# Identity products in TensorE's waits, at five places of a two-layer decoder kernel

## The reference

```
x = x + five SSM layers and one causal attention (16 heads of 64) of layernorm(x)
x = x + cross-attention (16 heads of 16) of layernorm(x) with the context
x = x + mixture of 8 experts, the two best of each token, of layernorm(x)
x = x + single-head self-attention of layernorm(x)
x = x + single-head cross-attention with four layernorms
x = x + int8-quantised product of layernorm(x) with a 256x256 matrix
```

## Time and profile before

| | us |
|---|---|
| median of three runs | 1249.07 (1248.18 to 1254.14) |
| profiled execution | 1250.04 |
| its span, first to last instruction | 1248.2 |
| TensorE matmul busy | 1113.7 (89%), 7155 records |
| VectorE busy | 795.8 (64%) |
| ScalarE busy | 707.1 (57%) |
| GpSimd busy | 714.3 (57%) |

### The profile page before, as it was taken

The page is one execution under the profiler, slowest core; times in us unless marked ns, Lnnn a source line. Parts: engine busy times, 40 slices in busy tenths (PEclk is TensorE's granted clock), DMA queues, the critical chain, the costliest instruction groups (busy, mean ns, idle before and its releaser), DMA issues.

```text
span 1248.2 us, 21861 instructions
## 1 busy us (share of the span) xinstructions
PE 1113.7 (89%) x7155; PEld 879.0 (70%) x7155; DVE 795.8 (64%) x1827; ACT 707.1 (57%) x2030; POOL 714.3 (57%) x776
## 2 busy tenths in 40 slices
PE   3999999999969999999988599984799999977983
PEld 3888888888857888888866477763466666656762
DVE  6778887888843666666675588876332333314795
ACT  2768777777833655555554588880223443225873
POOL 3598898989760225243353677760467555642664
PEclk9999999999989999999999899995899999998995
DMA  4201010000002000000020124610622222221001
GB/s 149 124 18 31 18 12 28 8 29 18 17 1 68 1 2 1 2 1 2 2 60 10 60 88 143 254 35 17 154 43 46 47 44 43 44 44 58 1 26 43
DMA packets 40225, 55.87 MB, mean 45 GB/s; under 512 B 8416, under 2 KB 35040, under 8 KB 38592
## 3 DMA queue, kind: packets, MB, share of 16 engines
q1 hardware_dynamic: 31392, 44.38, 10.9%
q0 software_dynamic: 8736, 10.25, 5.2%
HBM read 42.88 MB, written 11.74 MB: 44 GB/s over the span
## 4 chain that ended last, share of the span: by engine, by line
PE 45%; issue 7%; ACT 7%; DVE 7%; POOL 3%; DMA 1%; POOLq 0%; ACTq 0%; DVEq 0%
PE bank L1577 11%; PE bank L1594 5%; ACT x_prob L1244 4%; PE bank L44 4%; PE bank L46 3%; PE bank L45 3%; PE bank L704 2%; PE bank L732 2%; PE bank L715 2%; PE bank L1334 1%; PE bank L1586 1%; PE bank L1347 1%; PE bank L1284 1%; PE bank L2063 1%; POOL a_prob L871 1%
## 5 line engine op out<-in xcount | busy, mean ns | idle before, releaser
L440 DVE SCALAR_TENSOR_TENSOR ssm_conv<-bank,conv_w,ssm_conv 128x508 f32<-128x508 f32 (+2 forms) x240 | 160.8, 732 | 27.5 <-ACT ssm_conv L356 27.5
L765 ACT ACTIVATE a_prob<-a_prob,a_neg_max 128x128 f32<-128x128 f32 x256 | 99.7, 391 | 117.8 <-DVE a_neg_max L811 117.8
L1577 PE MATMUL bank<-expert_raw,x_kept_next_t 128*128 x312 | 148.7, 600 | 1.2 <-ACT x_kept_next_t L1656 1.2
L871 POOL TENSOR_TENSOR a_prob<-a_prob,a_inv 128x512 f32<-128x512 f32 x64 | 66.5, 1040 | 138.9 <-DVE a_inv L816 138.9
L552 POOL TENSOR_TENSOR ssm_u_lo<-ssm_conv,ssm_u_hi 128x512 fp32r<-128x512 f32 x80 | 101.4, 1289 | 27.0 <-ACT ssm_conv L366 26.9
L1521 POOL DMA_INDIRECT x_rows<-e_y,e_index x39 | 62.9, 1612 | 75.6 <-ACT e_y L1684 71.9
L1244 ACT ACTIVATE x_prob<-bank,x_neg_max 128x128 f32<-128x128 f32 x256 | 89.7, 401 | 11.5 <-DVE x_neg_max L1221 11.5
L1800 DVE COPY e_h_t<-bank 128x512 f32<-128x512 f32 x39 | 27.0, 691 | 105.4 <-PE bank L1586 105.4
L44 PE MATMUL bank<-w_out_hi,ssm_u_hi 128*128 128x256 f32 x320 | 92.1, 288 | 1.1 <-POOL ssm_u_lo L552 1.1
L1131 POOL TENSOR_TENSOR x_prob<-x_prob,x_inv 128x512 f32<-128x512 f32 x64 | 67.0, 1052 | 42.0 <-DVE x_inv L1225 41.5
L46 PE MATMUL bank<-w_out_hi,ssm_u_lo 128*128 128x256 f32 x320 | 90.8, 284 | 0.0
(11 more groups left out here) (338 smaller groups left out, 3264.4 us busy)
## 6 DMA issues: line engine op xcount, KB each, us to landing
expert_raw<-in_experts_laid SPq DMA_DIRECT2D x8, 1536.0 KB, 8.2
attn_raw<-in_attn_w_laid SPq DMA_DIRECT2D x1, 4096.0 KB, 12.4
w_in_raw<-in_L_attn_in_proj_w SPq DMA_DIRECT2D x5, 640.0 KB, 5.9
w_out_raw<-in_L_attn_out_proj_w SPq DMA_DIRECT2D x5, 512.0 KB, 3.9
x_res<-in_x SPq DMA_DIRECT2D x4, 512.0 KB, 5.5
x_res<-in_x SPq DMA_DIRECT2D x1, 2048.0 KB, 8.7
x_context<-in_ctx_t_laid SPq DMA_DIRECT2D x8, 256.0 KB, 4.0
z_rows<-x_kept_next_z SPq DMA_DIRECT2D x8, 256.0 KB, 2.2
```

What stands on the lines that cost most here:

```text
L440: op = dve.scalar_tensor_tensor(out=acc, in0=xs, scalar=conv_w[:, c, TAPS - 1 - back:TAPS - back], in1=acc, op0=ALU.mult, op1=ALU.add)
L765: e = act.activation(prob[:, m % 4, i, :], prob[:, m % 4, i, :], ACT.Exp, bias=neg_max[:, m % 4, i:i + 1], accum_out=total[:, m % 4, i:i + 1])
L871: pool.tensor_tensor(prob[:, t % 4, :, :], prob[:, t % 4, :, :], inv[:, t % 4, :].unsqueeze(2).broadcast_to([P, 4, P]), ALU.mult).then_inc ...
L1577: mm = pe.matmul(bank[:, :], rows_t[:, t % 2, k, :], W[:, bass.ds(at + (column + k * FFN), FFN)], start=(k == 0), stop=(k == KD - 1))
```

## The change

A function multiplies the 128x128 identity by itself, so many times, into a PSUM bank that nobody reads at that point. TensorE calls it at these places: after the attention outputs of tick 64 (8 products, with a wait for all masked scores ahead) and after the output projection of unit 30 (9); after the scores of the first cross-attention sequence (20, with a wait for the attention's sums ahead); in routing after the last sequence's probability transposes of r = 2 (4), its output projection (14), the last pair's transposes (3) and logits (18), the ranks (32) and the sum (26); at the hand-over after the three prepared products (18) and at the start of the second layer's block (21); and, by a table, after eight phases of the last pairs. Nothing else is changed: no other instruction is moved or removed, and no other engine's program differs.

```
--- before.py
+++ after.py
@@ -595,6 +595,13 @@
 WIDE = HEADS * HEAD
 KW = WIDE // P
 OCT = KW // 2
+
+
+def keep_at_work(pe, mem, bank, products):
+
+    ident = mem["ident"]
+    for _ in range(products):
+        pe.matmul(mem["psum"][bank][:, 0:P], ident[:, :], ident[:, :], start=True, stop=True)
 
 
 def stage_self_attention(nc, ctx, io, mem):
@@ -733,6 +740,9 @@
                                        v[:, s, head * HEAD:(head + 1) * HEAD], prob_t[:, (t - 1 + par) % 4, i, :],
                                        start=True, stop=True, tile_position=(0, par * HEAD))
                 mm.then_inc(ot_ready, 1)
+                if m == TICKS:
+                    pe.wait_ge(masked, TICKS)
+                    keep_at_work(pe, mem, 0, 8)
             unit = behind(m, OUT)
             if unit:
                 U, G, octet, s = unit
@@ -742,6 +752,8 @@
                     mm = product(pe, Y(U), [o_t_hi[:, U % 2, c, :], o_t_lo[:, c, :]], [x[:, octet * OCT + c, :] for x in wo],
                                  c == 0, c == OCT - 1)
                 mm.then_inc(y_ready, 1)
+                if U == TICKS // 2 - 2:
+                    keep_at_work(pe, mem, 0, 9)
             for half, j in jobs_at(m):
                 job(half, j)
             following(pe, m)
@@ -1309,6 +1321,8 @@
                     for s in range(PAIR):
                         tr = pe.transpose(psum[6][:, k * PT + s * P:k * PT + (s + 1) * P], next_z[:, s, k * P:(k + 1) * P], ident[:, :])
                 tr.then_inc(next_turned, 1)
+                if n == PAIRS - 1:
+                    keep_at_work(pe, mem, 3, 3)
             elif phase == "logits":
                 if n == 0:
                     pe.wait_ge(router_loaded, 16)
@@ -1318,6 +1332,8 @@
                         mm = pe.matmul(psum[6][:, s * EXPERTS:(s + 1) * EXPERTS], next_t[:, k, s * P:(s + 1) * P],
                                        router[:, k * EXPERTS:(k + 1) * EXPERTS], start=(k == 0), stop=(k == KD - 1))
                 mm.then_inc(logits_ready, 1)
+                if n == PAIRS - 1:
+                    keep_at_work(pe, mem, 3, 18)
             elif phase == "scores":
                 G, s = divmod(n, PAIR)
                 pe.wait_ge(k_copied, G + 1)
@@ -1336,6 +1352,9 @@
                                        tile_position=(r * ROWT, 0))
                         if c == KD - 1:
                             mm.then_inc(s_ready[r], 1)
+                if n == 0:
+                    pe.wait_ge(attention["y_added"], 2 * SEQS - 1)
+                    keep_at_work(pe, mem, 6, 20)
             elif phase == "turn_probs":
                 pe.wait_ge(prob_ready[r], n + 1)
                 copied = n * PAIR + r // 2
@@ -1346,6 +1365,8 @@
                 for i in range(4):
                     tr = pe.transpose(PT_BANK[r % 2][:, i * P:(i + 1) * P], prob[:, n % 2, r, i, :], ident[:, :])
                 tr.then_inc(pt_ready[r], 1)
+                if n == SEQS - 1 and r == 2:
+                    keep_at_work(pe, mem, 3, 4)
             elif phase == "outputs":
                 G, s = divmod(n, PAIR)
                 pe.wait_ge(v_copied, G + 1)
@@ -1370,6 +1391,8 @@
                 for k in range(KD):
                     mm = pe.matmul(Y, o[:, k, :], wo[:, k, :], start=(k == 0), stop=(k == KD - 1))
                 mm.then_inc(y_ready, 1)
+                if n == SEQS - 1:
+                    keep_at_work(pe, mem, 3, 14)
 
     phases = {
         "tensor": ("project_k", "project_v", "turn_z", "project_q", "scores", "turn_probs", "outputs", "project_o", "turn_next", "logits"),
@@ -1548,6 +1571,7 @@
                            either[:, b, :].unsqueeze(1).broadcast_to([P, SEQS - b, EXPERTS]),
                            start=False, stop=(b == SEQS - 1), skip_group_check=True)
         mm.then_inc(rank_ready, 1)
+        keep_at_work(pe, mem, 3, 32)
 
         pe.wait_ge(token_seq, 1)
         pe.wait_ge(token_lane, 1)
@@ -1556,6 +1580,7 @@
             mm = pe.matmul(SUM, lane_hot[:, n, :], token[:, n, :, :].rearrange("p a t -> p (a t)"),
                            start=(n == 0), stop=(n == CHOICES * SEQS - 1))
         mm.then_inc(sum_ready, 1)
+        keep_at_work(pe, mem, 3, 26)
 
         def turn_rows(t):
             pe.wait_ge(gathered[t % 3], 16 * (t // 3) + 16)
@@ -1637,6 +1662,7 @@
         for c in range(KD):
             mm = pe.matmul(SCALES[:, c * P:(c + 1) * P], ones[:, :], diag[:, c, :], start=True, stop=True)
         mm.then_inc(scales_ready, 1)
+        keep_at_work(pe, mem, 0, 18)
 
     def scalar(act):
         act.wait_ge(route_exp, 1)
@@ -1886,6 +1912,8 @@
     (456, "invert_o"), (462, "gain_o"), (475, "add_o"), (493, "norm_f"), (499, "measure_f"), (505, "invert_f"), (531, "scale_f"),
     (532, "quantise"), (532, "turn_f"), (544, "copy_f"), (571, "multiply"), (583, "store"), (675, "add_f"))}
 APART = 60
+BETWEEN = {("cscores", PAIRS - 2): 14, ("turn_cprobs", PAIRS - 2): 4, ("cscores", PAIRS - 1): 5, ("turn_cprobs", PAIRS - 1): 7,
+           ("multiply", PAIRS - 3): 10, ("turn_f", PAIRS - 2): 3, ("multiply", PAIRS - 2): 22, ("turn_f", PAIRS - 1): 2}
 
 
 def in_turn(*phases):
@@ -2047,6 +2075,7 @@
                     mm = pe.matmul(bank[:, s * D:(s + 1) * D], probs_t[:, s, :], vs(s), start=True, stop=True)
                 mm.then_inc(ready, 1)
 
+            keep_at_work(pe, mem, 0, 21)
             for phase, G in in_turn("turn_a", "project_q", "project_v", "scores", "turn_probs", "outputs", "turn_x", "cscores",
                                     "turn_cprobs", "coutputs", "turn_f", "multiply"):
                 if phase == "turn_a":
@@ -2114,6 +2143,7 @@
                             mm = pe.matmul(F[:, s * D:(s + 1) * D], xq_t[:, k * PAIR + s, :], wfq_t[:, k, :],
                                            start=(k == 0), stop=(k == KD - 1))
                     mm.then_inc(fy_ready, 1)
+                keep_at_work(pe, mem, 1, BETWEEN.get((phase, G), 0))
 
         @block.scalar
         def _(act):
```

## The result

The changed kernel takes 1241.64 us (median of five runs, 1241.41 to 1243.51), the kernel before 1249.41 us (five runs, 1248.18 to 1254.14). The ratio is 0.9932 with a 95% interval of 0.9914 to 0.995: faster by 0.7%, some 8 us, where some 13 us were forecast. The profiled execution has a span of 1239.7 us, 8.5 us less than before, and a mean granted clock of 0.985.

A forecast was written before the change was run, and what follows sets the result against it. Dependency chains in which PE takes its turns at 1.2 GHz were taken as the bound, ceiling 22.4 us. Terms 1.7 + 0 + 4.8 + 2.8 + 3.9 = 13.2 us gave a forecast of 1236.5 us, range 1231 to 1246.

The forecast's parts named there:

- rival (a): Whole kernel: every clock fall is only delayed or shortened, about half the gain is left, 6 us: 1243; chance 0.19.
- the price of a product: All fills: one product is two records, 0.22 us at 2.4 GHz and 0.44 us at 1.2 GHz.
- rival (c): All fills: records into one bank do not overlap, 0.55 us a product, some 50 us slower: 1300; chance 0.02.
- (e): Whole kernel: the products do not count for the clock, or PE is busy anyway; no change, 1249; chance 0.06.
- Self-attention's end: 8 and 9 products before 675.6 and 691.0: the half-clock stretch 676.75 to 680.17 vanishes, 1.7 us gained.
- hand-over: Between the layers, 18 and 21 products: transposes, query projection and value projection at full clock, 2.8 us gained.
- First scores: First cross-attention scores, 20 products: the clock falls a few microseconds later, is not spared, and the gain is 0.
- Routing: Six fills from outputs to gather: 3.2 us from shortened turns, 0.4 from ranks, 1.2 behind the sum, 4.8 us.
- the doubt: Routing behind the sum: thin PE work may let the clock fall, so the 26 products overrun; 1.2 of 2.2 us taken.
- The end of the second layer: Eight fills at the last pairs: transposes, outputs and last multiply at full clock, 1.7 + 1.3 + 0.9 = 3.9 us.
- (b): Routing from 844 on: fills begin at 1.2 GHz and overrun; +10 us, 1260; chance 0.08.
- (d): Whole kernel: the clock holds everywhere, 698 and 869 included, 15.8 us gained, 1234; chance 0.20.

The follow-up runs named there:

- scores_more: Changed kernel with 29 instead of 20 products behind the first cross-attention scores and 2 more behind each of the first two probability-transpose groups; 1239.75 us, ratio 0.9918.
- light_add: Changed kernel with GpSimd's last residual addition of pairs 3 and 4 done on 8 of 256 columns; 1238.9 us, ratio 0.9893.
- sum_fill: Changed kernel with two more products behind each of the first three groups of eight summing matmuls in routing; 1243.54 us, ratio 0.9938.
- the mends: Changed kernel plus products inside the sum, more at the first scores and second layer's start, and GpSimd's last additions later; all together 1232.37 us, ratio 0.9859.
- no_end: Changed kernel without the eight fills at the end of the second layer; 1242.78 us, ratio 0.9932.
- no_26: Changed kernel without the 26 products behind the routing's sum; 1244.4 us, ratio 0.994.
- add_late: Changed kernel with GpSimd's last additions moved behind its share of the output norm, and a third buffer; 1236.67 us, ratio 0.9885.
- no_end_add_late: Changed kernel with GpSimd's last additions moved late and without the eight fills at the second layer's end; 1239.11 us, ratio 0.9901.
- all_mended_2: Changed kernel with all four mends, and two end fills enlarged (9 for 5 and 20 for 10 products); 1232.93 us, ratio 0.9859.

## Why the prediction was right, and where it was not

**The number.** By the medians 7.8 us were won, where 12.6 us were forecast (1236.5). 1241.64 us lies nearer to rival (a), 1243, than to the forecast. The range of 1231 to 1246 held it, since it was drawn to hold (a) too. What was right is the mechanism and the terms up to the second layer's end, not the sum.

**What bounded the kernel, and the price of a product.** Right: dependency chains at half clock, and 0.23 us a product for 0.22 (40 records in 4.73 us). The products are not slower for sharing a bank, so rival (c) fell; and the clock answers to them (0.954 to 0.985), so (e) fell.

**Self-attention's end, hand-over.** Right: 1.6 us for 1.7, and 2.7 for 2.8. The ten other profiles with these products have 1.6 to 1.7 and 2.6 to 3.0 us, so neither is luck. The projection took 1.89 us, the query projection 1.99. The barrier was not held up: the first fill ended at 1116.6, and the second was 0.3 us ahead of what PE then waited for.

**First scores.** Right: the clock fell at 699.5 instead of 697.2 and cost what it had cost. scores_more shows the reason: with the 2.4 us that were left empty filled, and something in the two short waits behind them, the fall does not come.

**Routing.** 3.5 us for 3.6 up to the sum. Behind it, the doubt was right: the clock fell during the sum, the 26 products overran by 2.3 us (1.1 to 2.8 were named), and the full clock behind them won that back. I took 1.2 of 2.2 us for it; this profile had 0. Six other profiles with the same instructions there had 0, 1.5, 1.5, 1.5, 2.1 and 2.2 us. With this one their mean is 1.2, the value taken.

**The end of the second layer.** This step failed. The prediction added up half of PE's time on the chain at four places, 3.9 us, and 0.6 us came (0.2 us in the mean of five profiles). That PE was next on the chain was right, but the sum took VectorE's and GpSimd's durations as fixed. Two things were wrong. When PE hands over earlier, VectorE meets GpSimd in another place: its quantisations went from 1.38 and 0.61 us to 2.68 and 2.66 us, 3.35 us more. Other VectorE instructions met GpSimd at the same time or were freed of it (the addition `x_res<-x_res,l_o` of pair 7 went from 1.74 to 0.68 us), so that 2.4 us are left of it in all. That GpSimd's additions are the cause is shown by light_add, where they are small and the quantisations take 1.66 and 0.61 us. And even where VectorE's instructions stay as they are, with the additions late, the fills are worth 2.1 us and not 3.9: the term was also mis-sized. Which of its four places fell short was not taken apart.

The Trainium skill (SBUF — State Buffer, Who interferes with whom) says that VectorE's fast modes on SBUF data and GpSimd share a pair of ports, and that whoever comes second is blocked for the other's whole instruction. The rows agree: 0.3 us instructions ended with GpSimd's 1.3 us ones. The rule could have been weighed in the prediction, and was not.

**The rivals.** (a), falls only moved, is what happened in part: at 699, 867 and, in sum_fill, 877. (b) did not come; the longest low stretch after 710 was 6.8 us. Of the missing 5.5 us, 3.3 are the end, 1.2 the products behind the sum and 0.5 the cross-attention (0.3 of them in its steady part, unexplained); the rest is tenths of the other terms. (d), the clock held everywhere, is what the mends came near to: in scores_more it held at the scores and at the sum, for 1.6 us (against the changed kernel) and 2.2 us (against the kernel before). The last 0.8 us of the span's gain arose ahead of the change.

**The prediction's own arithmetic.** Three sums are a little off, and nothing hangs on them. With the 0.2 us of slack that it gives the 26 products, they would end 0.9 and 2.7 us late, not 1.1 and 2.8. The rest of the term behind the sum is 1.0 us and not the 1.2 of (d). And 240 products at 0.55 us in 62 us of waits overrun by 70 us, so that (c) is 56 us slower and not 50.

**Left open.** The runs of the kernel before lie in two groups, 1248.2 to 1251.4 and 1253.0 to 1254.4 us, and those with products do not spread that wide. The mean granted clock of each run is on record: 0.949 to 0.951 in the upper group, 0.950 to 0.957 in the lower, 0.949 and 0.954 in the mean. That is an estimated 12 us more at 1.2 GHz (0.005 of 1250 us, by the half clock) for some 5 us of time, so the upper group does lose more clock. In which place is not known, since no profile fell into it. Nor is it shown what sets the gather's 3.1 or 5.2 us, or why additions moved late win 2.5 us at the end without any fill. Each edit has one profile; where the falls of the clock wander, the ledgers above are samples of one.

## What to carry to other kernels

Where the low clock stretches a chain, fill the wait ahead of TensorE's next turn on it, with products whose sum at full clock is just under the wait, and with something in every thin stretch on the way, or the fall only moves. Price the overrun too: a fill that meets the low clock lasts twice as long and holds up what it was to speed up. And when a stage gets faster, lay the other engines' instructions over each other anew: here another engine's additions took back 2.4 us, and moving them later in the written order won 4.2 us by itself, about half of what the whole change did.

## What the runs showed of the hardware

The same instructions meet the clock in different places. In the stretch from 644 to 648 us, which no kernel changes, the clock fell in three profiles (the changed kernel, no_end, sum_fill) and in none of the ten others; it cost nothing, as the way to the first scores is the same. At 827 to 828 us, in the steady part of cross-attention, it fell for 3.4 us in five (no_26, light_add, add_late, no_end_add_late, all_mended_2), and there the way from the third scores to the outputs of sequence 14 was 0.7 to 1.1 us longer than before, against 0.0 to 0.3 us in the others. Behind the sum it fell in five of the seven profiles with the same instructions there, for 3.4 us in three and 6.8 us in two. The Trainium skill (TensorE: Matmul & The Clock Gate, Part 1) says that the monitor behind the clock runs freely and does not start with the kernel; these profiles agree.

VectorE's two quantisations of 128x256 values take together 0.61 us alone, 1.38 us with one operation of GpSimd beside them, and 2.68 us with two.
